# An interaction network on one core: four row tiles spread in one burst for half-width steps, and the fourth half-width block's first layer from DMA

## The reference

```python
xk = x0                                   # [batch, 32 fields, 16]
for W in (W0, W1, W2):                    # W: [32, h, 64]; h is 32, then 64, 64
    xk = relu(einsum('bmd,bhd,mhk->bkd', x0, xk, W))
    outs.append(sum(xk, axis=2))          # 64 features per layer
z = concatenate(outs)                     # 192 features
h = relu(concatenate([z, dense_ctx]) @ W_top1 + b_top1)
h = relu(h @ W_top2 + b_top2)
y = h @ W_top3
```

## Time and profile before

| | us |
|---|---|
| median of three runs | 345.42 |
| the runs | 343.63, 345.42, 345.49 |
| span of the profiled execution (no other time of it is shown) | 343.8 |
| TensorE busy, of the span | 311.0 (90%) |
| VectorE busy | 277.1 (81%) |
| GpSimd busy | 259.1 (75%) |
| ScalarE busy | 52.4 (15%) |

### The profile page before, as it was taken

One profiled execution on the slowest core, in us unless ns is written; L12 is line 12 of the kernel. 1 busy time (PEld: TensorE's weight loads), 2 busy tenths in 40 slices (PEclk: granted clock), 3 DMA queues, 4 the chain that ended last, 5 costly groups with the idle time before them and its releaser, 6 DMA issues.

```text
span 343.8 us, 4732 instructions
## 1 busy us (share of the span) xinstructions
PE 311.0 (90%) x1832; PEld 132.4 (39%) x1832; DVE 277.1 (81%) x174; ACT 52.4 (15%) x71; POOL 259.1 (75%) x199
## 2 busy tenths in 40 slices
PE   0198999998998989998989998999999999799997
PEld 0164564554564443332324432233333333233334
DVE  0039699699699999998999999989799969799420
ACT  1010100100101140321112101022122022020011
POOL 4677777777687989998889799899697859984000
PEclk9998999999999999999999999999999999999999
DMA  6176675464489799696889886947899995040000
GB/s 194 39 185 173 175 231 174 117 211 150 103 266 306 208 274 298 239 312 146 246 243 315 306 268 223 264 150 199 296 346 376 302 333 145 11 126 2 1 0 0
DMA packets 32529, 68.35 MB, mean 199 GB/s; under 512 B 5499, under 2 KB 12027, under 8 KB 32507
## 3 DMA queue, kind: packets, MB, share of 16 engines
q1 hardware_dynamic: 22074, 55.46, 48.6%
q10 hardware_dynamic: 6336, 11.54, 12.6%
q0 software_dynamic: 4096, 1.06, 3.5%
HBM read 54.40 MB, written 1.84 MB: 164 GB/s over the span
## 4 chain that ended last, share of the span: by engine, by line
PE 48%; DMA 14%; POOL 13%; issue 11%; DVE 10%; ACTq 1%; SPq 1%; ACT 0%; DVEq 0%; POOLq 0%
PE acc L878 36%; DVE vz L680 9%; POOL pz L628 7%; POOL gathered L602 6%; PE factor L845 4%; DMA fields_sb<-fields 4%; DMA rotated<-fields 4%; DMA hidden<-relu_out 3%; DMA fields<-gathered 2%; PE factor L890 2%; PE factor L823 1%; PE factor L885 1%; PE acc L874 1%; DVE feats L710 1%; ACTq L787 1%
## 5 line engine op out<-in xcount | busy, mean ns | idle before, releaser
L680 DVE TENSOR_TENSOR vz<-fields_sb,factor 128x1024 f32<-128x1024 f32 (+3 forms) x111 | 224.6, 2070 | 15.9 <-PE factor L823 6.2
L878 PE MATMUL acc<-vz,w_sb 128*64 128x512 f32 (+1 forms) x1200 | 222.7, 506 | 9.5 <-DVE vz L680 8.7
L602 POOL DMA_INDIRECT gathered<-in_table,index x128 | 121.8, 952 | 38.2 <-issue 30.6
L628 POOL TENSOR_TENSOR pz<-fields_sb,hidden 128x1024 f32<-128x1024 f32 (+1 forms) x60 | 132.5, 2231 | 12.6 <-DMA hidden<-relu_out 8.7
L878 PEld LDWEIGHTS acc<-vz,w_sb 128*64 128x64 f32 x1200 | 85.1, 139 | 129.5 <-issue 90.2
L878 PE MATMUL acc<-pz,w_sb 128*64 128x512 f32 (+1 forms) x240 | 57.4, 567 | 4.1 <-POOL pz L628 4.1
L776 ACT ACTIVATE relu_out<-acc 128x512 f32<-128x512 f32 (+1 forms) x30 | 15.3, 511 | 125.0 <-PE acc L878 90.7
L745 ACT ACTIVATE factor<-hidden 128x1024 f32<-128x1024 f32 x22 | 22.6, 1028 | 74.0 <-DMA hidden<-relu_out 59.9
L878 PEld LDWEIGHTS acc<-pz,w_sb 128*64 128x64 f32 x240 | 17.3, 137 | 36.2 <-issue 22.5
L680 DVE TENSOR_TENSOR vz<-rotated,factor 128x2048 f32<-128x2048 f32 x12 | 27.0, 2284 | 1.8 <-DMA rotated<-fields 1.7
L710 DVE TENSOR_REDUCE feats<-relu_out 128x32 f32<-128x512 f32 (+1 forms) x30 | 17.2, 574 | 8.0 <-ACT relu_out L776 8.0
(11 more groups left out here) (32 smaller groups left out, 61.3 us busy)
## 6 DMA issues: line engine op xcount, KB each, us to landing
fields_sb<-fields SPq DMA_DIRECT2D x48, 512.0 KB, 6.1
rotated<-fields SPq DMA_DIRECT2D x24, 512.0 KB, 5.4
hidden<-relu_out ACTq DMA_DIRECT2D x44, 256.0 KB, 6.3
fields_sb<-fields SPq DMA_DIRECT2D x32, 256.0 KB, 3.4
own<-fields SPq DMA_DIRECT2D x6, 512.0 KB, 3.9
gathered<-in_table,index POOLq DMA_INDIRECT x128, 4.4
fields<-gathered SPq DMA_DIRECT2D x12, 128.0 KB
w_sb<-in_w SPq DMA_DIRECT2D x2, 512.0 KB, 5.3
```

What stands on the lines that cost most here:

```text
L602: nc.gpsimd.indirect_dma_start(gathered[:, pair % GRING, j, :], None, table, bass.IndirectOffsetOnAxis(ap=index[:, i:i + 1], axis=0)).then ...
L628: nc.gpsimd.tensor_tensor(pz[:, at % PRING, 0:cols], fields[s][:, t, col:col + cols], hidden_of(step, g), ALU.mult).then_inc(pz_ready, 1)
L680: nc.vector.tensor_tensor(vz[:, at:at + nt, 0:cols].rearrange("p t (a n) -> p t a n", n=half), src[:, t:t + nt, col:col + cols].rearrange( ...
L878: last = nc.tensor.matmul(acc_of(step, ab), w_sb[layer][:, kt, :], z[:, ab * half:(ab + 1) * half], start=start and j == 0, stop=stop and ...
```

## The change

It has three parts.

**Bursts.** A step in `SPREAD` now has one spread on TensorE that sends all four matmuls (g = 0 and 1, a and b) behind each other and signals once. `spread_free` is the later of the two entries' free points, so the burst stands where the spread of g = 1 could stand. VectorE, ScalarE's copy and the relu wait for this one signal.

**Block 3.** `DIRECT` loses block 3. Its layer 0 comes by DMA like that of full-width blocks: two scratch copies, `own`, `opposite` and four `rotated`, all of half width, and a `put` on ScalarE; VectorE makes two products and GpSimd the opposite one. `opposite` gets a place for each half, and the gathers that reuse the buffers of its pair wait for GpSimd's product. Steps that take a turn with block 2 keep their waits through `HALVES` and `second_half`.

**Tables.** `POOL_TILES`, `FIRST_GATHERS`, `GATHERS_IN`, `PACED` and `LOADS` are new. GpSimd's tiles change at (2, 2) from 4 to 2, (1, 5) 4 to 1, (2, 4) 2 to 4, (1, 6) and (1, 7) 4 to 3, (2, 6) 5 to 6, (2, 7) 6 to 5. The opposite product of (0, 3) stands behind 40 gathers, 31 more stand behind it and ahead of the first product of (2, 2). In `LOADS` block 3's operands follow its scratch copies, its fields go behind block 4's scratch copies, and block 4's operands behind block 5's.

```diff
+HALVES = [b for b, block in enumerate(BLOCKS) if block[2] == N]
-DIRECT = (0, 1, 2, 3)
+DIRECT = (0, 1, 2)
-POOL_TILES = {(1, 0): 0, (2, 0): 0, (1, 1): 0, (2, 1): 0, (1, 2): 0, (2, 2): 4, (1, 3): 0, (2, 3): 4,
-              (1, 4): 4, (1, 5): 4, (2, 4): 2, (2, 5): 4, (1, 6): 4, (1, 7): 4, (2, 6): 5, (2, 7): 6,
-              (1, 8): 6, (1, 9): 6, (2, 8): 4, (2, 9): 3}
-FIRST_GATHERS = 27
-GATHERS_IN = {(2, 2): (43, 0, 0, 1), (0, 4): (12,), (2, 3): (0, 1, 0, 0), (1, 4): (4, 2, 1, 0),
-              (1, 5): (1, 1, 0, 2), (0, 6): (3,), (2, 4): (1, 1), (2, 5): (5, 2, 3, 1), (0, 7): (5,),
-              (1, 6): (3, 1, 2, 1), (1, 7): (0, 4, 0, 0), (2, 6): (1, 0, 0, 0, 0)}
+POOL_TILES = {(1, 0): 0, (2, 0): 0, (1, 1): 0, (2, 1): 0, (1, 2): 0, (2, 2): 2, (1, 3): 0, (2, 3): 4, (1, 4): 4,
+    (1, 5): 1, (2, 4): 4, (2, 5): 4, (1, 6): 3, (1, 7): 3, (2, 6): 6, (2, 7): 5, (1, 8): 6, (1, 9): 6, (2, 8): 4,
+    (2, 9): 3}
+FIRST_GATHERS = 40
+GATHERS_IN = {(2, 2): (31, 0), (0, 4): (12,), (1, 4): (6, 0, 1, 1), (1, 5): (4,), (0, 6): (2,), (2, 4): (4, 1, 1,
+    0), (2, 5): (5, 2, 1, 1), (0, 7): (5,), (1, 6): (3, 0, 3), (1, 7): (0, 4, 0), (2, 6): (1, 0, 0, 0, 0, 0)}
...
-LOADS = [('scratch', 0), ('fields', 0), ('scratch', 1), ('fields', 1), ('scratch', 2), ('fields', 2), ('scratch', 3), ('fields', 3), ('scratch', 4), ('operands', 4), ('scratch', 5), ('operands', 5), ('fields', 4), ('fields', 5), ...
+LOADS = [('scratch', 0), ('fields', 0), ('scratch', 1), ('fields', 1), ('scratch', 2), ('fields', 2), ('scratch',
+    3), ('operands', 3), ('scratch', 4), ('fields', 3), ('scratch', 5), ('operands', 4), ('operands', 5),
+    ('fields', 4), ('fields', 5), ...
     for step, g in FACTORS:
+        if step in SPREAD and g == 1:
+            continue
+def spread_free(step):
+
+    return max(factor_free((step, g)) for g in range(HHALF))
 def spread_after(step, g):
-    return max(factor_free((step, g)), min(vectors_to(source(step)) + 1, VECTOR.index((step, 0))))
+    return max(spread_free(step), min(vectors_to(source(step)) + 1, VECTOR.index((step, 0))))
...
+                if second_half(b):
+                    sp.wait_ge(own_in[s], operands_in(b - 1))
...
-                sp.dma_start(opposite[s][:, :], far).then_inc(opposite_in[s], 16)
+                if second_half(b):
+                    sp.wait_ge(opposite_in[s], operands_in(b - 1))
+                sp.dma_start(opposite[s][:, at:at + quarter], far).then_inc(opposite_in[s], 16)
...
-            def spread(step, g):
-
-                before, half = source(step), BLOCKS[step[1]][2] // 2
+            def spread(step):
+                before = source(step)
                 pe.wait_ge(relu_done, ORDER.index(before) + 1)
-                if factor_free((step, g)):
-                    pe.wait_ge(vz_ready, factor_free((step, g)))
-                for ab in range(2):
-                    row = ab * HID + g * HROWS
-                    last = nc.tensor.matmul(factor_of(step, g)[:, ab, :], unit_sb[row:row + HROWS, :],
-                                            relu_of(before)[row:row + HROWS, :], start=True, stop=True)
+                if spread_free(step):
+                    pe.wait_ge(vz_ready, spread_free(step))
+                for g in range(HHALF):
+                    for ab in range(2):
+                        row = ab * HID + g * HROWS
+                        last = nc.tensor.matmul(factor_of(step, g)[:, ab, :], unit_sb[row:row + HROWS, :],
+                                                relu_of(before)[row:row + HROWS, :], start=True, stop=True)
                 last.then_inc(factor_spread, 1)
```

More of the change, by code:

```diff
@@ L94 @@
 IN_FLIGHT_DIRECT = 3
-LOADS = [('scratch', 0), ('fields', 0), ('scratch', 1), ('fields', 1), ('scratch', 2), ('fields', 2), ('scratch', 3), ('fields', 3), ('scratch', 4), ('operands', 4), ('scratch', 5), ('operands', 5), ('fields', 4), ('fields', 5), ('scratch', 6), ('operands', 6), ('scratch', 7), ('operands', 7), ('fields', 6), ('fields', 7), ('scratch', 8), ('operands', 8), ('scratch', 9), ('operands', 9), ('fields', 8), ('fields', 9)]
+LOADS = [('scratch', 0), ('fields', 0), ('scratch', 1), ('fields', 1), ('scratch', 2), ('fields', 2), ('scratch',
+    3), ('operands', 3), ('scratch', 4), ('fields', 3), ('scratch', 5), ('operands', 4), ('operands', 5),
+    ('fields', 4), ('fields', 5), ('scratch', 6), ('operands', 6), ('scratch', 7), ('operands', 7), ('fields', 6),
+    ('fields', 7), ('scratch', 8), ('operands', 8), ('scratch', 9), ('operands', 9), ('fields', 8), ('fields', 9)]
 def fields_order(b):
@@ L450, in landed, with second_half @@
             return 16 * (turn(b) + 1)
+        def second_half(b):
+            return b not in DIRECT and b - 1 not in DIRECT and BLOCKS[b - 1][0] == BLOCKS[b][0]
         def relay_count(step):
@@ L538, in field_tiles @@
                                    [[0, HROWS], [cols, MREP], [1, cols]])
-                    if b - 1 in DIRECT and stream(b - 1) == s:
+                    if b in HALVES and stream(b - 1) == s:
                         sp.wait_ge(fields_in[s][t], landed(b - 1))
@@ L589, in gather @@
                     for a in range(before):
-                        if BLOCKS[a][0] == pair - GRING:
+                        if BLOCKS[a][0] == pair - GRING and a in DIRECT:
                             pool.wait_ge(vz_ready, vectors_to((0, a)))
+                        elif BLOCKS[a][0] == pair - GRING:
+                            pool.wait_ge(pz_ready, pools_to((0, a)))
                     pool.wait_ge(scratch_in[stream(before)][0], landed(before))
@@ L607, in opposite_product @@
                 _, col, cols, _, _ = BLOCKS[step[1]]
-                s, quarter = stream(step[1]), cols // QUART
+                s, quarter, at = stream(step[1]), cols // QUART, col // QUART
                 pool.wait_ge(opposite_in[s], operands_in(step[1]))
@@ L611, in opposite_product @@
                     pool.wait_ge(pz_used, pools_used_to((0, step[1] - 1)))
-                nc.gpsimd.tensor_tensor(oz[:, 0:quarter], quarter_rows(step[1]), opposite[s][:, :],
+                nc.gpsimd.tensor_tensor(oz[:, 0:quarter], quarter_rows(step[1]),
+                                        opposite[s][:, at:at + quarter],
                                         ALU.mult).then_inc(pz_ready, 1)
@@ L667, in product @@
                 if step in SPREAD:
-                    dve.wait_ge(factor_spread, SPREADS.index((step, g)) + 1)
+                    dve.wait_ge(factor_spread, SPREADS.index((step, 0)) + 1)
                     if g == 1 and step in COPIED:
@@ L754, in copy_hidden @@
             def copy_hidden(step, g):
-                act.wait_ge(factor_spread, SPREADS.index((step, g)) + 1)
+                act.wait_ge(factor_spread, SPREADS.index((step, 0)) + 1)
                 if pools_read(step):
@@ L770, in relu @@
                     if (layer + 1, b) in SPREAD:
-                        act.wait_ge(factor_spread, SPREADS.index(((layer + 1, b), 1)) + 1)
+                        act.wait_ge(factor_spread, SPREADS.index(((layer + 1, b), 0)) + 1)
                     elif layer < 2:
@@ L910, in _ @@
                 elif who == "spread":
-                    spread(step, u)
+                    spread(step)
                 else:
@@ L974 @@
     ids = np.array(inputs["ids"]).reshape(PAIRS, QUART, GATHERS, FIELDS)
-    for pair in {BLOCKS[b][0] for b in DIRECT}:
+    for pair in {BLOCKS[b][0] for b in HALVES}:
         ids[pair] = (ids[pair].reshape(2, 2, 2, GATHERS // 2, FIELDS).transpose(0, 2, 1, 3, 4)
```

12 lines of the change are left out of this document (7 added, 5 removed), and 10 rows, old and new, of the table PACED.

## The result

Before 345.41 us (343.63 to 345.49, four runs), after 350.27 us (349.66 to 356.65, four runs). The ratio is 1.0149, 95% interval 1.0108 to 1.0190. The forecast was 345.2 us in a range of 341.0 to 348.2: two us outside, on the slower side; its sign was left open, with 0.26 for slower. The profiled execution took 349.66 us with a span of 347.9, 4.1 us more than the old span of 343.8. All that follows is in these spans.

A forecast was written before the change was run, and what follows sets the result against it. Half-width blocks were taken as some 16 us bound by VectorE and 9 by PE and VectorE in turn. Shifts ran +2.0, -0.8, +2.8, +2.0, +3.6, +1.4, +1.0 to -0.2: span 343.6, median 345.2 us, range 341.0 to 348.2.

The forecast's parts named there:

- Part 1: Bursts at half-width steps and (1,7): VectorE's factor comes 1.0 us later at (2,0) and (2,1), +2.0 for the two.
- Part 2: Block 3's layer 0 from DMA: VectorE loses three gaps, 3.1 us; (2,2) begins at 90.6 against 91.42, -0.8.
- Part 3: POOL's order around block 3: held 2.7 us for the opposite rows, its product late; (1,3) +2.8, (2,3) +2.0.
- (1,3) begins 3.5 us after p: After VectorE's ring of nine tiles fills: slot 1.35 us, v55 1.75, a sum 0.4; (1,3) at 101.7, +2.8.
- p: POOL's first product of (2,2): ready at 98.2, wanted by PE at 93.9, so PE waits 4.3 us.
- v55: VectorE's product number 55 in program order, where its ring is full; slot free 1.35 us after p.
- The covers of block 4: Operands in by 105, wanted at 111; fields land by 127, wanted at 132: covers of 6 and 5 us.
- Part 4: Tables from (1,5) on: shift +3.6 at (2,4), +1.4 at (1,6), +1.0 at (2,6), -0.2 behind it.
- A: Rival: POOL is not held, block 3's rows land by 55.5, p ready at 95.9; 342.8 us, chance 0.24.
- B: Rival: POOL is held longer, block 3's rows land at 60.3, all behind moves by 2.3; 347.5 us, chance 0.15.
- C: Rival: VectorE bounds from (1,5) on, half of the vanished waits (1.7 and 2.6) stay; 347.4 us, chance 0.13.
- D: Rival: PE's busy time bounds the kernel, 8.6 us less; 336.8 us in full, 341 with half, chance 0.10.

The follow-up runs named there:

- bursts_only: The kernel before with the bursts alone, block 3 still direct and all tables as before: 347.52 us, 1.0079 of the kernel before.
- pe_filled: The changed kernel with eleven matmuls on constant data put on TensorE ahead of its first GpSimd product of (2,2): 353.75 us, 1.0245 of the kernel before.
- operands4_first: The changed kernel with block 4's operands ahead of block 5's scratch copies in `LOADS`: 351.72 us, 1.0166 of the kernel before.
- both: operands4_first with gathers moved: (2,2) has 24, (0,4) 15, (1,4) 10 in place of 31, 12, 6: 347.19 us, 1.0060 of the kernel before.
- later_tables: The kernel both with the earlier kernel's `POOL_TILES` from (1,5) on, its gathers and a fitting `PACED`: 347.72 us, 1.0073 of the kernel before.

## Why the prediction was wrong

The forecast span was 4.3 us too short. By stretches, from the table of shifts:

| stretch | forecast | measured | beyond the forecast |
|---|---|---|---|
| to (1,3) | +2.8 | +5.0 | +2.2 |
| (1,3) to (2,3) | -0.8 | -0.9 | -0.1 |
| (2,3) to (2,4) | +1.6 | +2.7 | +1.1 |
| (2,4) to (1,6) | -2.2 | -1.9 | +0.3 |
| (1,6) to (2,6) | -0.4 | +1.0 | +1.4 |
| (2,6) to the end | -1.2 | -1.8 | -0.6 |

**Part 1, the bursts: right.** VectorE's wait went from 0.35 to 1.25 us at both places, +0.9 each where I had +1.0. bursts_only alone costs 2.4 us by its median, with three such waits, where this part had +2.0 for two.

**Part 2, block 3 from DMA: right in direction.** The gap of 2.10 is gone, (2,2) begins at -1.7 (forecast -0.8).

**The step that failed: Part 3's "(1,3) begins 3.5 us after p".** That POOL comes late and PE waits was right: p was ready at 98.3 (forecast 98.2), and PE waited 5.12 us where I had 4.3, since PE came to it 0.6 us sooner. But (1,3) began 5.5 us after PE took p, not 3.5. The sum counts what follows the wait at the times of the rows of before, 0.60 and 1.03 us for four and eight matmuls. PE's granted clock had fallen to its half level inside the wait, they took 1.12 and 1.92, the slot of v55 was free 2.9 us after p instead of 1.35, and VectorE then stood another 0.52 us while the burst of (1,3) ended at 103.74. pe_filled, at full clock, has the 3.6. This is the largest of the misses above, 2.0 of the 2.2 us to (1,3). That POOL's late product as a whole costs most of the time is shown by operands4_first and both: on one chip, with block 4's operands ahead in `LOADS`, seven gathers moved from ahead of it, four of them behind block 4's opposite product too, give back 3.7 to 4.5 us.

**Luck in Part 3.** The opposite rows landed at 58.00, as forecast to the tenth, but the same transfer landed between 59.00 and 60.91 in every other profile of a kernel with this layer 0 on the chips of 345 us. POOL stood 1.19 us for them, not 2.7, having lost 1.65 us at its pacing wait at 27.16 (1.95 with the 0.30 of every gather), which my sum did not have. The Trainium skill (DMA: Bandwidth & Descriptors, Anatomy of one DMA) gives about 2.0 us and the bytes over 436 GB/s for DMAs on GpSimd's path; these rows go over SyncE's queue, and the 64 KB issued until 55.12 were there 2.9 us later, so the measured time decides. Nor do the 0.7 us of stop that I wrote for that figure follow from it: an estimate by it from my own 55.0 is a landing at 57.2 and a stop of 1.9.

**The covers of block 4 held, the "+1.5" for the fields of block 5 did not.** VectorE waited for no operand and no field of block 4. I had counted each cover by itself, though they are one queue: both blocks' operands took from 90.92 to 111.0, 20 us where I had 15.4 from block 4's 7.7 us before. Before, the queue had a slack of 7.5 us of waiting for VectorE, which I never read; it took up part of the delay, and the scratch copies of block 6 came 5.9 us late, not 1.5. In the kernel after, this shows up as 0.79 us ahead of 149.46, where before had a wait of 0.17 for a slot. The other 0.7 us between (2,3) and (1,4) are a wait of 0.88 for PE ahead of block 5's rotated product. Whether the queue would set the time once POOL is early, no run separates.

**Part 4, the later tables: right up to (1,6), wrong behind it.** From (1,5) to (2,4) the new kernel takes 1.4 us more than the old one (18.1 against 16.8), forecast 1.6: the three tiles (+3.3) and the vanished rotated wait (-1.7). Up to (1,6) 1.9 us come back (2.2 forecast). From there to (2,6) I left 0.3 of VectorE's 2.9 us of idle time; the new kernel has 2.0 of them, all at (2,6), where VectorE still waits for PE's slot. later_tables says that the new tables as a whole are no loss.

**Rivals.** A did not come to pass. B did in other executions. C, that half of the waits that I let vanish stay, was right in its second half: of 2.6 us 1.7 stayed, while the wait for rotated tiles went. D, PE's busy time as the bound, was furthest off: 4.3 us less work, 4.1 us more time. My own sign of being wrong, that PE's idle time would not rise by some 8 us, did not come: it rose by 8.4. PE's busy time was 306.7 and not 302 to 303: the half clock on 3.9 us of work makes about 2.0 of the difference, and bursts_only shows 1.3 less saved by the bursts than I had. An aggregate can agree while the step that carries the end is wrong.

**Open.** The last 2 us of both. The operands of block 5 still wait there for scratch copies that end at 97, and (2,4) is late by 3.4; no experiment separated that from the waits for GpSimd's tiles in block 4. What the half clock costs at the end of the kernel is open too.

## What to carry to other kernels

A wait on TensorE may cost more than its length, so count what follows it at the granted clock of a row that stood behind such a wait. When an edit that undoes a cause returns nothing, look in its trace for a new wait of its own before calling the cause innocent. Read a queue's own waits before moving work in it: a stretch where it waits for its consumer is the slack of everything behind it, and one sum over the whole queue is needed, not one cover per transfer.

## What the runs showed that I had not expected

- In a wait of 5.12 us on TensorE, behind full work, the granted clock fell to its half level (1.2 GHz) about 2.2 us after the last matmul and stayed there for 6.8 us, 3.9 of them on the work behind the wait. Waits of 7.64 and 7.99 us in other kernels had the same fall, for about 10 us. Waits of 2.92 and 1.68 us at places near by did not.
- The landing of the same 64 KB of opposite rows lay at 58.00 in the profile of after and at 59.00 to 60.91 in nine others, and on one chip alone at 59.00 and 60.91. In the one at 60.44 the own rows that go ahead of them were issued at 56.15 instead of 53.53, 1.5 us of it because the scratch copies went later and 1.1 because they took longer.
- Two of the chips ran the kernel before in 382 to 385 us instead of 345; the profiles taken there have TensorE standing still for up to 8.4 us at a time with no engine in the record that releases it.
